# A layer norm's scale and shift on ScalarE in place of VectorE, in a fused window-attention kernel

## The reference

```
xn = (x - m) * rsqrt(v + 1e-5) * norm1_g + norm1_b    # m, v over the 128 channels of a token
xw = windows(roll(xn, (-4, -4)))                      # 64 windows of 8 x 8 tokens
q, k, v = split(xw @ qkv_w.T + qkv_b)                 # 16 heads of 8 channels
q, k = rope2d(q), rope2d(k)
attn = softmax(q * scale @ k.T + attn_mask)
x = x + roll(merge(attn @ v) @ proj_w.T + proj_b, (4, 4))
h = layer_norm(x) @ fc1_w.T + fc1_b                   # second layer norm, gated MLP
x = x + (silu(gate) * a) @ fc2_w.T + fc2_b
out = gamma * attention(x) + x
```

## Time and profile before

| | us |
|---|---|
| runs | 462.19, 460.42, 461.11 (median 461.11) |
| profiled execution, its own time | 459.28 |
| its span, first to last instruction | 457.5 |
| TensorE busy | 380.5 (83%) |
| VectorE busy | 352.0 (77%) |
| ScalarE busy | 271.0 (59%) |
| GpSimd busy | 254.5 (56%) |

### The profile page before, as it was taken

The page is one execution under the profiler, slowest core; times in us unless marked ns, Lnnn a source line. Parts: engine busy times, 40 slices in busy tenths (PEclk is TensorE's granted clock), DMA queues, the critical chain, the costliest instruction groups (busy, mean ns, idle before and its releaser), DMA issues. The chain is left out here.

```text
span 457.5 us, 11279 instructions
## 1 busy us (share of the span) xinstructions
PE 380.5 (83%) x4148; PEld 202.0 (44%) x4148; DVE 352.0 (77%) x830; ACT 271.0 (59%) x424; POOL 254.5 (56%) x303
## 2 busy tenths in 40 slices
PE   0448699999999999882997999999688897989684
PEld 0224465565665666562454555554233242342231
DVE  7977578889888888865545666652889989899896
ACT  2532867787787778781422333333687858768460
POOL 7775657677777868667392444420005747747510
PEclk9999889999999999995897999999769999999999
DMA  8300001010110100100000000000000000010011
GB/s 293 111 14 18 19 26 30 25 29 23 29 29 23 32 26 26 32 6 0 0 2 2 1 0 0 1 2 0 0 0 1 0 23 26 0 47 0 0 47 47
DMA packets 10951, 11.32 MB, mean 25 GB/s; under 512 B 3591, under 2 KB 8488, under 8 KB 10792
## 3 DMA queue, kind: packets, MB, share of 16 engines
q1 hardware_dynamic: 9680, 9.45, 6.6%
q10 hardware_dynamic: 1240, 1.46, 0.9%
HBM read 4.61 MB, written 2.10 MB: 15 GB/s over the span
## 5 line engine op out<-in xcount | busy, mean ns | idle before, releaser
L1203 POOL TENSOR_TENSOR el<-e,eh 128x1024 f16<-128x1024 f32 x24 | 51.0, 2125 | 56.0 <-DVE eh L1408 56.0
L1082 POOL TENSOR_TENSOR p_lo<-e_buf,p_hi 128x1024 f16<-128x1024 f32 x32 | 68.2, 2131 | 5.3 <-ACT p_hi L922 3.7
L1477 ACT ACTIVATE e_sum<-ps,mq 128x1024 f16<-128x1024 f32 x32 | 35.6, 1114 | 19.0 <-DVE mq L1379 19.0
L314 PE MATMUL ps<-y_t,fc_w 128*128 128x512 f16 x192 | 46.6, 387 | 0.0
L978 ACT ACTIVATE e_buf<-ps 128x1024 f32<-128x1024 f32 x32 | 32.7, 1023 | 18.1 <-PE ps L716 18.1
L886 DVE TENSOR_REDUCE ps<-ps 128x16 f32<-128x1024 f32 x32 | 39.4, 1232 | 5.2 <-PE ps L704 4.4
L695 PE MATMUL ps<-mask,identb 128*128 (+1 forms) x128 | 40.3, 398 | 3.1 <-DMA k_t<-qk_t 2.9
L1249 PE MATMUL ps<-eh,val 128*128 128x512 f16 x128 | 33.1, 381 | 10.9 <-POOL el L1203 7.5
L1074 POOL TENSOR_TENSOR rot<-ta,tb 128x256 f32<-128x256 f32 x32 | 23.3, 728 | 33.5 <-DVE tb L867 33.4
L322 PE MATMUL ps<-hid,fc_ws 128*128 128x512 f32 x64 | 36.2, 648 | 5.3 <-DVE hid L413 5.2
L1418 DVE TENSOR_REDUCE mx<-ps 128x1 f32<-128x1024 f32 x32 | 38.8, 1212 | 0.0
(11 more groups left out here) (154 smaller groups left out, 941.9 us busy)
## 6 DMA issues: line engine op xcount, KB each, us to landing
k_t<-qk_t SPq DMA_DIRECT2D x128, 32.0 KB, 1.8
x_all<-in_x SPq DMA_DIRECT2D x8, 256.0 KB, 5.5
out<-ob SPq DMA_DIRECT2D x8, 256.0 KB, 2.0
mask_f<-in_mask ACTq DMA_DIRECT2D x1, 1024.0 KB, 8.3
fc_w<-in_fc_w SPq DMA_DIRECT2D x1, 512.0 KB, 9.4
fc_w<-in_fc_w SPq DMA_DIRECT2D x1, 256.0 KB, 9.0
qkv_w<-in_qkv_w ACTq DMA_DIRECT2D x1, 192.0 KB
proj_w<-in_proj_w ACTq DMA_DIRECT2D x1, 64.0 KB
```

The costliest lines, as they stand in the source:

```text
L314: last = pe.matmul(ps[:, bank, :], fc1_w16[:, ws, 128 * block_:128 * block_ + 128], y_t[:, v, ys, :], start=(n == 0), stop=(n == 2))
L1082: pool.tensor_tensor(p_lo[:, u], e_buf[:, u], p_hi[:, u], ALU.subtract).then_inc(plo_done, 1)
L1203: eng.tensor_tensor(el[:, key % H_BUFS, :], e4[:, key % E_BUFS, :], eh[:, key % H_BUFS, :], ALU.subtract).then_inc(el_done, 1)
L1477: act.activation(e_sum[:, m % 2, :], two(s_bank(m - 1, cur)), ACT.Exp, bias=mq[:, m - 1:m], scale=1.0, accum_out=den[:, v, m - 1:m]).then_ ...
```

## The change

The four scale-and-shift operations of each chunk leave VectorE's list. ScalarE takes them into `ln_hi_of`, as four activations with the identity function whose scale and bias are per-partition operands, ahead of the copy to float16. ScalarE now waits for GpSimd's `ln_rstd` itself, and then for its own four activations. Nothing else is changed; the values are the same numbers.

```diff
-                def ln_norm_of(c):
-
-                    dve.wait_ge(ln_rstd, c + 1)
-                    if c >= 2:
-                        dve.wait_ge(ln_lo, c - 1)
-                        dve.wait_ge(ln_hi, c - 1)
-                    for k in range(TPC):
-                        last = dve.tensor_scalar(xn[:, c % 2, 128 * k:128 * k + 128], x_all[:, TPC * c + k, :],
-                                                 rstd[:, c, k:k + 1], nmr[:, c, k:k + 1], ALU.mult, ALU.add)
-                    last.then_inc(ln_norm, 1)
-
...
                 def ln_hi_of(c):

-                    act.wait_ge(ln_norm, c + 1)
+                    act.wait_ge(ln_rstd, c + 1)
                     if c >= 2:
                         act.wait_ge(ln_turned, c - 1)
                         act.wait_ge(ln_lo, c - 1)
+                    for k in range(TPC):
+                        last = act.activation(xn[:, c % 2, 128 * k:128 * k + 128], x_all[:, TPC * c + k, :],
+                                              ACT.Identity, bias=nmr[:, c, k:k + 1], scale=rstd[:, c, k:k + 1])
+                    last.then_inc(ln_norm, 1)
+                    act.wait_ge(ln_norm, c + 1)
                     copy(xh[:, c % 2, :], xn[:, c % 2, :]).then_inc(ln_hi, 1)
```

More of the change, by code:

```diff
@@ L823, in _ @@
                 dve.tensor_scalar(gains[:], g1b1[:], WSCALE, None, ALU.mult).then_inc(gains_ready, 1)
-                ln_norm_of(0)
                 ln_stats_of(2)
-                ln_norm_of(1)
                 ln_stats_of(3)
@@ L830, in _ @@
                 dve.tensor_tensor(b_sum[:], ps[0:33, S_BANK, 0:3 * DIM], qkv_b[:], ALU.add).then_inc(qkv_b_ready, 1)
-                ln_norm_of(2)
                 dve.wait_ge(qkv_b_ready, 1)
@@ L838, in _ @@
                 dve.tensor_tensor(mrest[:, 0], mask_f[:, 0], mask16[:, 0, 0], ALU.subtract).then_inc(mask_rest, 1)
-                ln_norm_of(3)
                 ln_stats_of(EARLY + 1)
@@ L851, in norm @@
                         dve.tensor_copy(mask_any[0:1, :], ps[0:1, S_BANK, 0:1]).then_inc(mask_known, 1)
-                    ln_norm_of(c)
                     if c + 1 < CHUNKS:
```

## The result

The changed kernel takes 465.15 us (median of 6 runs, 463.62 to 467.53) against 461.12 for the kernel before (6 runs, 460.14 to 462.19): ratio 1.0096, 95% interval 1.0072 to 1.012, so +4.4 us (3.3 to 5.5). The forecast was 466.0, slower by 5.0.

A forecast was written before the change was run, and what follows sets the result against it. Hand-overs between engines bound the first 60 us, TensorE the first attention from there. Seven groups, 11.3 us less 6.3 covered, add 5.0 to the median 461.11: 466.1, rounded to 466.0; range 462.0 to 468.8.

The forecast's parts named there:

- the turn of k: TensorE's turn of k behind chunk 7, at 55.40 us before; forecast near 60.4, its +5.0 us carried to the end.
- The size of the group: Four ScalarE activations per chunk: 474 ns each, overlapping by 0.10 us, 1.61 us together; bounds 1.0 and 1.90.
- Seven on the chain: Seven groups of 1.61 us delay the pipeline, 11.3 us, 6.3 covered by waits; each 0.1 us per group costs 0.7.
- the walk: Chunk-by-chunk tracing of hand-overs from chunk 0 to 7, with xl shifts of +2.13 (chunk 3) to +4.98 us (chunk 7).
- the branch: TensorE's work beginning when chunk 4's turn is released; taken as 3.52 us, with ScalarE's group 5 beside it.
- The fifth group: Chunk 5's activations on ScalarE, beside TensorE's 3.52 us branch: claimed to cost nothing, with 0.3 us to spare before rot.
- GpSimd's wait for the statistics: GpSimd's wait for VectorE's mean and variance: should shrink from 7.8 us to nearly nothing beyond the first.
- B: Rival: operands of consecutive ScalarE activations are free, a group lasts 1.0 us; 462.0 us, no change; chance 0.10.
- D = 1.0: Here the assumed duration of one ScalarE group, 1.0 us, the lower bound with operands fetched for nothing; forecast used 1.61.
- C: Rival: VectorE's early statistics free GpSimd, so xl of chunks 3, 4, 6 start 3.3 us sooner; 457.8 us; chance 0.04.
- D: Rival: ScalarE activations fetching two operands do not overlap, a group lasts 1.90 us; +7.0, 468.1 us; chance 0.13.
- E: Rival: GpSimd's delay behind chunk 7 does not reach TensorE, late only by +2.5 to +3.0; 464.0 us; chance 0.07.

The follow-up runs named there:

- its own kernel: Kernel before, with only the scale-and-shift group of chunk 7 moved to ScalarE: ratio 1.0064 (1.0041 to 1.0088), +2.9 us.
- early statistics alone: Kernel before, with VectorE's statistics of chunks 4 to 7 ahead of the preceding chunk's scale and shift, nothing moved to ScalarE: ratios 0.9957 and 0.9979.
- the last kernel: Kernel before with those early statistics, plus ScalarE's copies to xn_all of chunk 6 and xh of chunk 7 ahead of the first p_hi: 456.1 us, ratio 0.9904.

## Why the prediction was right, point by point

- The forecast (+5.0 us, slower with a chance of 0.86) held: +4.4 and +5.4 us in two measurements. The sizes of the steps were read from the trace of before alone. That +5.0 lies in the middle of the two is luck: they differ by 1.0 us from each other, and the profiles have +5.7 and +5.5 at the turn of k.
- The size of the group: 4 activations were to last 1.61 us, they last 1.64, and one 481 ns where 474 was built from a bare one and the difference of 173 ns. With copies instead, the group lasts 0.90, the lower bound.
- Seven on the chain: that the loss goes with the length of the group is shown by the kernel with copies and the one with the group twice, for chunk 7 by its own kernel's profile. The number seven rests on the shifts of the walk, found one by one in the profile, and on a slope between 6 and 8; each of the other six was not moved alone. That a group behind xn_all is the cause, and not ScalarE's load, is shown by the kernel with the group moved ahead.
- The walk was short by 0.7 us at the turn of k: 0.3 at the start (ScalarE's table load began at 6.75 instead of 5.84 us in this execution, and the first group at 8.15 instead of 7.89), 0.1 in the branch (3.64 us instead of 3.52), and some 0.05 in each of the groups and hand-overs. In the second profile the same turn is at 60.92, +5.5.
- The fifth group: in the profiles hidden, as said, while the timed runs lean towards a cost of about 1 us, and it stays open. The spare time I named (0.3 us to rot) was not its whole cover: with the group twice, its 1.3 us did not show either.
- GpSimd's wait for the statistics was to shrink to nearly nothing beyond the first. It shrank from 7.8 to 4.3 us: the wait for chunk 7's stayed (2.54 us), because these statistics stand behind the row maximum of the step, before and after. It is a miss without a price, since xh was later still.
- The rivals: B's walk (+0.9 at D = 1.0, so +0.2 at the 0.90 that its group lasted) agrees with the kernel that had such a group (-1.2 to +0.3). C's mechanism exists, at 1 to 2 us of its 3.3, and in this change it is part of the cover that the walk had counted. D did not occur (a group lasts 1.64 us, not 1.90), nor E (TensorE still waits 2.43 us for k, 5.7 us later).

## What to carry to other kernels

An engine with idle time can still be the wrong place for an operation: look at what stands ahead of it and behind it in the engine's own list, and walk the chain, group by group, with the waits that cover it. The same 32 activations cost 4 to 5 us behind a copy that waits for another engine. One place earlier, in that wait, the kernel is as fast as before, and 0.6 to 1.6 us, hardly clear of noise, slower than with early statistics alone. An operation with two per-partition operands on ScalarE lasted 481 ns at 128 columns where a bare one took 301. Bare ones took 301 ns at 128 columns and 1023 at 1024, so an estimate for the data of 128 columns is 103 ns: in these tiles the two operands, with the identity in place of a copy, weigh more (180) than the data.

## What the runs showed of the hardware

- TensorE's step up in clock fell at another place in each execution. From the turn of q of pair 0 to that of pair 1 (39.51 and 46.05 before) it is 6.54 us in the kernel before, 7.22 in its copy with one more semaphore, 6.18 and 7.20 in two executions of the changed kernel, and 4.79 with the group twice. In the slower ones the masks and the first scores of that step took 1.02 to 1.07 us each, where the first execution of the changed kernel had 0.60 to 0.63. The granted clock shows this step up only in the copy with one more semaphore (0.50, then 1.00 from 45.7 us on); in the other four it reads 1.00 all along, so there the step is read from the durations. This alone moves a single profile by about 1 us, as do the branch (3.36 to 4.02 us over the profiles) and the start (xh(0) of VectorE's kernels between 9.22 and 10.23). Shifts of 1 us are to be read between two rows of one profile.
- Behind the turn of k TensorE began at a granted clock of 0.50 in every profile but one, with 0.60 or 0.61 us for four transposes and 1.06 for the first mask, after an idle time of 1.9 to 2.4 us. In the last kernel it was idle for 1.61 us and went on at its higher level (granted clock 1.00, rows of 0.40 and 0.59 us). Four rows of that step at 1.03 to 1.06 instead of 0.6 to 0.7 us make 1.7 of the 2.1 us by which its first reciprocal follows sooner. The length of the last idle time does not decide alone: with the group twice, TensorE was idle for only 1.17 us ahead of 58.90 and its transposes took 0.61; the granted clock had fallen at 57.5 already, before this idle time began, and 1.0 us behind the end of one of 1.78 us. What decides was not tried apart.
- In the kernel before a VectorE scale and shift took 332 ns with GpSimd idle (29.85) and 862 to 1176 where it began beside an xl (10.29, 17.75, 22.80, 28.09), and xl 2.04 us instead of 1.15 beside mrest (16.81). With xn on ScalarE, the 32 activations of the changed kernel last 477 to 489 ns and show no such stretching.
